# Last stage of a three-stage tower: the products of the end tile's first half three steps later, the turned keys behind one set of exponentials

## What is computed

```python
gating = softmax(x @ W_gate.T)                      # x = layernorm(h), 16 heads
indicator = one_hot(argmax(gating), 16)
q, k, v = split(x @ W_qkv.T, 3)
k_shared = einsum("bth,bthd->btd", indicator, k)     # one key and value row of 32 features
v_shared = einsum("bth,bthd->btd", indicator * max(gating), v)
att = softmax(causal(q_h @ k_shared.T / sqrt(32)))   # 16 query heads, 192 x 192 each
h = h + concat_h(att @ v_shared)
```

## Time and profile before

| | us |
|---|---|
| median of 3 runs | 1246.56 |
| lowest, highest | 1246.15, 1249.61 |
| the profiled execution | 1243.13 |
| its span, first to last instruction | 1241.3 |
| mean granted TensorE clock | 0.983 |

### The profile page before, as it was taken

How to read it: one execution, slowest core, us unless ns; L and a number is a source line. 1 busy time by engine, 2 the same in 40 slices (tenths; PEclk the granted TensorE clock), 3 DMA queues, 4 the chain that set the end, 5 groups by cost and what they waited for, 6 DMA issues and landing times.

```text
span 1241.3 us, 24152 instructions
## 1 busy us (share of the span) xinstructions
PE 1145.6 (92%) x8880; PEld 954.9 (77%) x8880; DVE 794.5 (64%) x1547; ACT 538.9 (43%) x1713; POOL 517.6 (42%) x714
## 2 busy tenths in 40 slices
PE   1689999999999999979999999998999999999995
PEld 1577878888788888758788878777887878778885
DVE  7898867768678553264556554643667667667665
ACT  6334334443344422253443333232565555555654
POOL 3577766766667672043233323312032232132231
PEclk9989999999999999989999999999999999999997
DMA  7022222222222222697776554516427266275161
GB/s 276 26 94 94 85 110 99 106 110 86 111 95 110 102 102 85 235 300 196 216 232 192 165 143 128 154 51 128 96 57 170 57 130 139 50 163 117 47 143 43
DMA packets 67301, 156.44 MB, mean 126 GB/s; under 512 B 12528, under 2 KB 30064, under 8 KB 65648
## 3 DMA queue, kind: packets, MB, share of 16 engines
q1 hardware_dynamic: 67184, 154.90, 42.7%
HBM read 68.50 MB, written 57.02 MB: 101 GB/s over the span
## 4 chain that ended last, share of the span: by engine, by line
PE 74%; DVE 13%; ACT 4%; issue 3%; POOL 2%; DMA 2%; SPq 1%; DVEq 0%; POOLq 0%; ACTq 0%
PE psum L823 24%; PE psum L1377 10%; PE psum L2204 10%; PE psum L2195 5%; PE psum L2254 4%; PE psum L2242 3%; PE psum L798 2%; PE psum L1333 2%; PE psum L2237 1%; PE psum L1354 1%; PE psum L1362 1%; PE psum L1318 1%; PE psum L2234 1%; SPq L1732 1%; DVE turn L520 1%
## 5 line engine op out<-in xcount | busy, mean ns | idle before, releaser
L1837 ACT ACTIVATE probs<-psum,row_max 128x128 f32<-128x128 f32 (+1 forms) x384 | 142.8, 386 | 70.2 <-DVE row_max L2000 67.9
L1119 ACT ACTIVATE square_scratch<-psum 128x128 f32<-128x128 f32 x192 | 51.0, 278 | 145.5 <-PE psum L1355 145.5
L2133 POOL TENSOR_TENSOR h_rows<-h_rows,y_normed 128x512 f32<-128x512 f32 x24 | 30.8, 1284 | 180.2 <-DVE y_normed L2017 180.2
L2000 DVE TENSOR_REDUCE row_max<-psum 128x2 f32<-128x384 f32 (+1 forms) x128 | 76.8, 600 | 41.6 <-PE psum L2244 23.7
L2111 POOL TENSOR_TENSOR picked_rows<-picked_rows 128x768 f32<-128x768 f32 (+1 forms) x64 | 61.4, 960 | 95.7 <-DVE picked_rows L1982 92.0
L753 POOL TENSOR_TENSOR stage<-stage 128x512 f32<-128x512 f32 x48 | 81.1, 1711 | 37.5 <-DVE stage L629 37.5
L1295 POOL TENSOR_TENSOR rr<-ss,consts_r 128x3 f32<-128x3 f32 x64 | 14.6, 228 | 188.9 <-ACT square_scratch L1119 184.8
L798 PE MATMUL psum<-m,basis 128*128 128x64 f32 x384 | 49.1, 284 | 33.5 <-DVE basis L280 27.4
L1377 PE MATMUL psum<-wo_high,y_high 128*128 128x512 f32 x192 | 79.2, 412 | 0.9 <-issue 0.9
L1201 DVE SCALAR_TENSOR_TENSOR s_t<-psum,consts_r 128x384 f32<-128x384 f32 (+1 forms) x128 | 55.7, 478 | 37.0 <-PE psum L1333 31.7
L1837 ACT ACTIVATION_READ_ACCUMULATOR probs<-psum,row_max 128x1 f32 x384 | 79.1, 206 | 0.0
(11 more groups left out here) (275 smaller groups left out, 3461.7 us busy)
## 6 DMA issues: line engine op xcount, KB each, us to landing
qk<-stage SPq DMA_DIRECT2D x24, 512.0 KB, 2.6
v<-stage SPq DMA_DIRECT2D x24, 512.0 KB, 2.6
g<-gate_rows SPq DMA_DIRECT2D x24, 512.0 KB, 2.6
qk_rows<-qk SPq DMA_DIRECT2D x16, 512.0 KB, 6.8
q_stack_even<-q_t_high SPq DMA_DIRECT2D x32, 224.0 KB, 4.8
q_stack_even<-q_t_low SPq DMA_DIRECT2D x32, 224.0 KB, 6.7
q_stack_odd<-q_t_high SPq DMA_DIRECT2D x32, 224.0 KB, 5.5
q_stack_odd<-q_t_low SPq DMA_DIRECT2D x32, 224.0 KB, 6.6
```

Of the source, the lines that this page charges most:

```text
L1119: last = nc.scalar.activation(sqs[:, h % 2, t], psum[:, OB[h % 3], t * RV:(t + 1) * RV], ACT.Square, accum_out=ss[:, h % 2, t:t + 1])
L1837: last = nc.scalar.activation(pr[:, g % 2, c], psum[:, s_bank(g), c], ACT.Exp, bias=mx[:, g % 3, x:x + 1], accum_out=dsum[:, t, h:h + 1])
L2000: V.reduce_max(mx[:, g % 3, 0:nh], psum[:, s_bank(g), 0:nh * w].rearrange("p (h n) -> p h n", h=nh), AX, negate=True).then_inc(s_max.sem, 1)
```

## The change

In the first seven pairs the products of the end tile's first half, `values(i, 2)`, are issued in step 15 in place of step 12: in TensorE's order behind `scores` of the next pair's second group and ahead of `logits(i + 2)`. ScalarE's `kt_evac` is issued in step 13 behind `exps(14)`, in place of step 12 ahead of `norm(i + 2, 2)`. And `turn` of a pair's first group waits for two product blocks of the pair before in place of three (its place in the buffer was last read by the second block); groups 1 to 3 wait for three, as before. The last pair's own tuple is unchanged, and no instruction is added or removed.

```diff
@@ -1615,7 +1615,7 @@
     SB_LAST = [0, 1, 6]
-    VALUES, VALUES_LAST = (4, 8, 12), (6, 10, 13)
+    VALUES, VALUES_LAST = (4, 8, 15), (6, 10, 13)
     YB = [2, 3, 4, 5]
@@ -1688,7 +1688,7 @@
         i, n = divmod(g, NS_F)
-        return y_sum.at(i - 1, 3) if n < 4 else y_sum.at(i, (0, 1, 2)[(n >= 7) + (n >= 12)])
+        return y_sum.at(i - 1, 3 if n else 2) if n < 4 else y_sum.at(i, (0, 1, 2)[(n >= 7) + (n >= 12)])
@@ -1856,7 +1856,7 @@
                     logits_exp(i + 1)
-                if n == 12:
+                if n == 13:
                     kt_evac(i + 1)
```

## The result

The changed kernel takes 1250.55 us (median of 14 runs, 1247.62 to 1254.01), the kernel before 1246.01 us (14 runs, 1242.71 to 1250.59). The ratio is 1.0038, with a 95% interval of 1.0026 to 1.0051: 4.5 us slower. The profiled execution of the changed kernel has a span of 1249.2 us against 1241.3, so the two profiled executions lie further apart (7.9 us) than the medians.

What follows compares the result with a forecast made beforehand. TensorE was taken as the bound, with pairs 1 to 4 held by the queries' DMA landing. Terms -1.34 + 2.7 - 1.55 = -0.2, plus three clock falls of +4.8, gave +4.6 us on 1246.6: 1251.2 us, range 1243.5 to 1256.0.

Steps and rivals of the forecast that it cites:

- The bound: TensorE's first scores of pairs 2 to 5 wait for the landing of the stacked queries' 16 DMA transfers.
- The gap paid twice: Pairs 1 to 4: TensorE waits 1.55 us longer for the queries, and the 0.68 us behind stay: +2.7 us.
- The clock: Longer waits in pairs 1 to 4 lower TensorE's granted clock: three falls at 1.6 us, +4.8 us.
- the sum without falls: All pairs' terms with no clock fall counted: -1.34 + 2.7 - 1.55 = -0.2 us.
- pair 2's fall: Clock fall behind pair 2's wait of about 2.3 us, nearest to lengths that go either way; three falls were taken.
- six cases of a fall: Six idle stretches of TensorE of 1.93 us and longer in the profile; the granted clock fell in all six.
- The keys' wait: Turned keys come out later, ahead of `x_transposes`: 0.2 us of new wait (0 to 0.4) where no DMA wait swallows it.
- rival 3: Wait for the turned keys is 0.9 us, showing in pairs 0 and 5 only: +1.4 us; a term, no chance given.
- Pairs with time to spare: Pairs 0 and 5, without a wait for the queries: -1.55 + 0.2 + 0.68 = -0.67 us each.
- The last pair: Pair 6's work comes sooner and ends the last pair's 2.22 us wait earlier: -1.55 us.
- Rival 2: The queries' landing does not hold; pairs 0 to 5 gain 0.67 us, pair 6 1.55: 5.6 us, 1241.0; chance 0.12.

Runs made afterwards that it cites:

- the run with filler: Changed kernel with eight repeated mask matmuls in the wait for the stacked queries ahead of the first scores of pairs 2 to 5: 1247.27 us, ratio 1.0019.
- ten fillers: Changed kernel with ten useless mask matmuls (2.2 us) in the wait for the queries ahead of the first scores of pairs 2 to 5: 1244.65 us, ratio 0.9995.
- the run with only the free pairs changed: Changed kernel with late products and late turned keys only in pairs 0, 5 and 6, pairs 1 to 4 as before: 1243.16 us, ratio 0.9989.
- the old count: Changed kernel with the load behind the stacked queries, the turn of a pair's first group waiting for the late products again: 1234.95 us, ratio 0.9911.

## Why the prediction was right

**The bound.** That the scores of pairs 2 to 5 wait for DMA was an inference from a difference of 0.1 us. It is shown by three things: the waits of the run with filler name the transfers; the waits grew by 1.2 to 1.8 us, 1.5 in the mean, about the time by which TensorE comes sooner (2.59, 2.29, 3.34 and 2.24 us against the 2.7, 2.3, 3.1 and 2.6 predicted); and moving the load, by which the transfers of pairs 1 and 2 start 3.9 and 3.3 us sooner after their mark, ended them.

**The gap paid twice.** Predicted for the stretch from step 3 of pair 1 to step 3 of pair 6 without falls: 4 x 0.68 - 0.67 = +2.05 us. Measured with the clock held up: +1.97. By itself the stretch behind the first scores grew by 0.6 us in place of 0.68.

**The clock.** Predicted: 1.6 us a fall and three of four, the step that carried the sign. Measured: 1.6 us a fall, and four of four in the profiled execution; 2.05 + 4 x 1.6 = 8.5 is just what that stretch lost. The medians moved by 4.5 only, where four falls would have made it 6.2. With ten fillers the median is 0.8 below the kernel before, against the -0.2 of the sum without falls. So part of the falls seems to be in the median of before. Two things on record speak for that. A wait like pair 3's falls at times without the change, as it did in the run with only the free pairs changed, while the profiled execution of the kernel before shows none. And the mean granted clock of every run is known: 0.9822 in the mean of the 68 runs of the kernel before that stand beside the experiments (0.977 to 0.986), 0.9786 in that of the changed kernel's 14, 0.9836 in that of the 12 with ten fillers. A fall takes 0.21 x 8 us of some 1246, 0.00135, so the changed kernel and the one before lie an estimated 2.7 falls apart and not four, and the one with ten fillers has about one fall fewer than the kernel before. Where in the execution they fell is not known for runs without a profile.

Some of the closeness of +4.6 to +4.5 is therefore luck. The forecast left out pair 2's fall, as its wait was the shortest; in the profile the clock fell there as well. What brings the medians back to about three falls seems to be that the kernel before has some of its own, which the forecast did not weigh. One of its six cases of a fall was also misread: ahead of the last pair's 2.22 us wait the clock was already down.

```profile
1214.00:1217.00 3.00, 1.00 (x5) 0.77 (x5) 2.20 (x4) 3.00 (x18) 0.00 (x0) 0.50 0.52 133
```

So the count was five of five.

The Trainium skill's section (TensorE: Matmul & The Clock Gate, Part 1: The HAM clock gate) names an idle window as what halves the clock. Taken strictly, a pause with work on both sides would leave the clock high; the four falls behind waits of 2.2 to 3.3 us don't bear that reading out. Its sentence that the place of a transition varies from run to run is about the rise, and agrees in kind: behind one and the same idle time the clock fell in some profiled executions only (last section).

**The keys' wait** was the wrong term, of about the right size. Predicted: 0.2 us for the turned keys. In its place 0.3 us for VectorE's pick, which I had not looked at because TensorE had always come 1.5 us later. The copy is done when the transposes start (in pair 2 it ends at 1009.13, their loads start at 1009.45). The mechanism of rival 3 is real all the same: a row maximum 1.3 us later brings it out.

**Pairs with time to spare.** Predicted 0.67 us each, measured 0.74 with the landing moved, 0.70 in pair 5 (47.36 us before, 46.66 after, from its step 3 to pair 6's), and 0.76 in pair 0 (from the first transposes of its output rows, at 892.99 before and 893.50 after, to the first mark). That the first mark is only 0.25 us ahead comes from the stages before, which ran 0.5 us later in this execution.

**The last pair.** Predicted -1.55 us. Its first products do start sooner: 41.56 us after the mark of pair 6 against 43.15, 1.59 won, the idle time ahead of them 1.33 us in place of 2.22 (under 1 us was forecast). Only 0.4 us of it reached the end, since the last products of all now run behind a fall of the clock. Timeline of PE, changed kernel, then the kernel before:

```profile
1223.89 1.93 PE L2254 MATMUL psum<-raw_f,v_spread_odd 32*32 32x128 f32 x80 [1.33 <-issue]
...
1238.75 2.81 PE L2254 MATMUL psum<-probs_t_odd,v_spread_odd 32*32 32x128 f32 x88 [2.46 <-DVE probs_t_odd L2008]
1242.25 1.11 PE L2275 MATMUL psum<-ident,y_heads_t 128*128 128x128 f32 x4 [0.69 <-ACT y_heads_t L1844]
```

```profile
1232.15 1.59 PE L2254 MATMUL psum<-probs_t_odd,v_spread_odd 32*32 32x128 f32 x88 [2.17 <-DVE probs_t_odd L2008]
1234.43 1.11 PE L2275 MATMUL psum<-ident,y_heads_t 128*128 128x128 f32 x4 [0.69 <-ACT y_heads_t L1844]
```

The same 88 matmuls take 2.81 us in place of 1.59. Whether this fall belongs to the change or to the single execution is open; in the profiled executions of the other versions it comes in some and not in others.

**Rival 2** priced at 5.6 us what the change gives where the landing does not bind. That is what it gave once the load was moved: 1238.80 to 1233.39, 5.4 us.

## What to carry to other kernels

Before work is moved from one gap of an engine's queue to another, ask what ends the gap that it leaves: if that is a transfer, the work was free cover, and it costs its full length at its new place less the idle time that it fills there. When a wait in front of TensorE grows towards 2 us, add the price of a clock fall behind it; a few idle matmuls into a bank that is about to be overwritten show in one run how much of a loss is clock. And look at what feeds the transfer: here one load moved behind the queries in SyncE's queue turned a change of +4.5 us into one of -5.4 (each against the kernel without the change and with the same queue).

## What the hardware showed that was not expected

A matmul that computes nothing was worth its time: ten of them in each of four waits took 5.4 us off the median, by the ratios 1.0038 and 0.9995. In pairs 1 to 4 a fall has one price, 0.79 over 8 us and 1.6 us of time (in the runs with eight and with no fillers). But it has no sharp edge in the idle time alone. Ahead of the loads of L2167 near 815 us all 14 profiled executions have the same idle time, 1.93 or 1.94 us, and the clock fell behind it in two of them, that of the kernel before and that with the old count. In the changed kernel it stayed up:

```profile
813.60:821.60 8.00, 5.39 (x36) 4.47 (x35) 6.20 (x12) 6.25 (x12) 1.43 (x4) 1.00 0.47 131
```

In pairs 1 to 4, 1.77 and 1.79 us left the clock at 1.00, 1.99 us did not, and all of 2.31 us and above brought a fall. In the last pair even some 2.5 us did not always: with the load late the changed kernel has 2.54 us of idle time between loads, up to 1221.3, and a clock of 1.00 in the 6 us from there:

```profile
1221.00:1227.00 6.00, 2.24 (x92) 1.74 (x92) 1.18 (x3) 0.60 (x1) 1.26 (x1) 1.00 0.11 39
```
